# Cross-attention prologue: x loaded a second time with features on partitions, query weights centred on the chip, the layer norm's scale applied in the query eviction

## The reference, cut to what matters

```python
def _layernorm(x, axis=-1, eps=1e-05):
    m = jnp.mean(x, axis=axis, keepdims=True)
    v = jnp.var(x, axis=axis, keepdims=True)
    return (x - m) / jnp.sqrt(v + eps)
...
q = rms_norm(linear(h, q_w, q_b), norm_q_w)
...
x = x + _L0_xattn_ref(_layernorm(x, axis=-1), ctx_2048, ...)
x = x + _L0_ffn_ref(_layernorm(x, axis=-1), ...)
```

## Time and profile before

| | us |
|---|---|
| median of three runs (1572.07 to 1576.45) | 1574.91 |
| the profiled execution, its own time | 1576.47 |
| its span | 1574.7 |
| TensorE busy | 1532.1 (97%) |
| VectorE, ScalarE, GpSimd busy | 1190.8, 711.5, 702.1 |

### The profile page before, as it was taken

How to read it: one execution, slowest core, us unless ns; L and a number is a source line. 1 busy time by engine, 2 the same in 40 slices (tenths; PEclk the granted TensorE clock), 3 DMA queues, 4 the chain that set the end, 5 groups by cost and what they waited for, 6 DMA issues and landing times.

```text
span 1574.7 us, 41288 instructions
## 1 busy us (share of the span) xinstructions
PE 1532.1 (97%) x16250; PEld 1192.2 (76%) x16250; DVE 1190.8 (76%) x1884; ACT 711.5 (45%) x1457; POOL 702.1 (45%) x786
## 2 busy tenths in 40 slices
PE   8999999999999999999999999999997999999997
PEld 6776777777777777777777777777775787777997
DVE  5763788878888888888878888788888586554986
ACT  5763444443444444444434444434445124555441
POOL 5762444344444344444344443444446592113752
PEclk9999999999999999999999999999999999999999
DMA  6853111112211112111122111122114524011000
GB/s 190 238 161 128 47 55 56 49 49 70 70 49 55 49 51 78 60 50 53 49 66 69 54 54 49 49 69 71 49 36 125 190 107 161 27 36 46 1 1 24
DMA packets 66167, 113.70 MB, mean 72 GB/s; under 512 B 21392, under 2 KB 36080, under 8 KB 64576
## 3 DMA queue, kind: packets, MB, share of 16 engines
q1 hardware_dynamic: 65280, 110.20, 22.1%
q0 software_dynamic: 832, 2.75, 0.6%
HBM read 82.59 MB, written 30.34 MB: 72 GB/s over the span
## 4 chain that ended last, share of the span: by engine, by line
PE 90%; ACT 6%; DVE 2%; issue 1%; POOL 1%; DMA 0%; SPq 0%; ACTq 0%
PE ps L1466 22%; PE ps L1467 19%; PE ps L1468 19%; PE ps L1607 8%; PE ps L1573 6%; PE ps L1548 3%; PE ps L1519 3%; PE ps L1579 2%; PE ps L1818 2%; ACT prob L801 2%; PE ps L1801 2%; PE ps L1810 1%; PE ps L1501 1%; ACT prob L799 1%; PE ps L1583 1%
## 5 line engine op out<-in xcount | busy, mean ns | idle before, releaser
L547 POOL TENSOR_TENSOR prob_img<-prob 128x448 f32<-128x448 f32 x128 | 150.8, 1178 | 216.1 <-ACT prob L801 216.1
L510 POOL TENSOR_TENSOR ctx_lo<-ctx_raw,ctx_hi 128x472 fp32r<-128x472 f32 (+1 forms) x62 | 111.6, 1819 | 244.5 <-ACT ctx_hi L742 244.5
L1108 DVE RECIPROCAL rec<-ps 128x224 f32<-128x224 f32 x128 | 199.0, 1555 | 6.0 <-PE ps L1607 2.3
L799 ACT ACTIVATE prob<-ps 119x448 f32<-119x448 f32 x128 | 69.7, 545 | 196.0 <-PE ps L1573 196.0
L1097 DVE TENSOR_REDUCE top<-ps 112x4 f32<-112x1028 f32 x128 | 156.1, 1219 | 0.0
L1102 DVE SCALAR_TENSOR_TENSOR prob_img<-prob,ones_last,prob_img 23x448 f32<-23x448 f32 x128 | 87.5, 683 | 76.4 <-POOL prob_img L547 74.3
L775 ACT ACTIVATE sq_junk<-proj 128x513 bf16<-128x513 f32 (+1 forms) x96 | 61.1, 637 | 173.3 <-DVE proj L1076 173.3
L1096 DVE TENSOR_REDUCE top<-ps 112x4 f32<-112x472 f32 x128 | 82.9, 648 | 61.3 <-PE ps L1548 61.3
L1573 PE MATMUL ps<-q_all,k_all 32*128 32x112 f32 (+1 forms) x3072 | 125.7, 274 | 0.0
L801 ACT ACTIVATE prob<-ps 128x896 f32<-128x896 f32 x128 | 116.9, 914 | 0.0
L1466 PE MATMUL ps<-w_v_img_hi,ctx_hi 128*128 128x512 f32 x256 | 109.7, 428 | 0.0
(11 more groups left out here) (331 smaller groups left out, 4394.8 us busy)
## 6 DMA issues: line engine op xcount, KB each, us to landing
ctx_raw<-in_ctx_dram SPq DMA_DIRECT2D x32, 748.0 KB, 4.2
xh_dram<-xh SPq DMA_DIRECT2D x32, 448.0 KB, 3.1
q_dram<-q_turned SPq DMA_DIRECT2D x28, 256.0 KB, 2.8
q_all<-q_dram SPq DMA_DIRECT2D x32, 224.0 KB, 3.1
out_dram<-out_sb SPq DMA_DIRECT2D x32, 224.0 KB, 2.3
xh<-in_x_dram SPq DMA_DIRECT2D x31, 224.0 KB, 2.8
xa<-in_x_dram SPq DMA_DIRECT2D x21, 256.0 KB, 3.6
ring<-in_wo_dram SPq DMA_DIRECT2D x2, 2048.0 KB, 8.8
```

Source lines behind the costliest of these rows:

```text
L510: nc.gpsimd.tensor_tensor(ctx_lo[:, :, cols], ctx_raw[:, :, cols], ctx_hi[:, :, cols].bitcast(F32), ALU.subtract).then_inc(ctx_lo_done, 1)
L547: nc.gpsimd.tensor_tensor(prob_img[:, g % 2], prob[:, g % 2, 1, :], prob[:, g % 2, 2, :], ALU.add).then_inc(img_summed, 1)
L799: nc.scalar.activation(prob[0:CHUNK_C, g % 2, 0, :].rearrange("p (j q) -> p j q", j=GH), ps[0:CHUNK_C, 2:6, 0:L], ACT.Exp).then_inc(exp_do ...
L1108: nc.vector.reciprocal(rec[:], bank[:, 2:4]).then_inc(norm_step, 1)
```

## The change

The host program also passes `xT`, x with features on partitions, one tile of 128 tokens contiguous for each partition. SP loads it to one of three buffers `xc`, besides the rows, which go to one of two buffers `xa` and serve only for mean and variance. The turns of x, the GpSimd normalisation and its shift are gone. TensorE makes the mean of the query weights over features by four full-precision products with a constant of 1/512; VectorE subtracts it from the staged weights (`centre`). The eviction of a query tile multiplies by the token's inverse spread and adds the bias. The query turn of tile k-2 stands between the two halves of the products of tile k; ScalarE's copy of it comes one iteration later, behind the squares of tile k-1. The expansions of `pick_rows` move from the start to k = 12 and 14.

```diff
-        xa = [qp(f"xa{e}", [P, D])[:] for e in range(3)] + [proj[:, 1, 0:D]]
+        xc = [qp(f"xc{e}", [P, D])[:].rearrange("p (c l) -> p c l", c=KC) for e in range(3)]
+        xa = [proj[:, e, 0:D] for e in range(2)]
+        mean_w = q_turned[0][:, 0, :]
...
+            def load_xc(t_):
+                sp.dma_start(xc[t_ % 3], t["xT"][t_]).then_inc(xc_loaded[t_ % 3], 16)
...
             def pre():
                 sp.sem_inc(out_stored, 16)
+                load_piece(0)
+                load_xc(0)
+                load_piece(1)
                 load_xa(0)
+                sp.dma_start(pick_rows[:], t["pick_rows"]).then_inc(pick_loaded, 16)
+                load_xc(1)
+                sp.dma_start(q_bias[:], t["q_b"].partition_broadcast(P)).then_inc(q_bias_loaded, 16)
                 load_xa(1)
...
+                load_xc(2)
...
                 for k in range(NT + 2):
-                    if k + 4 < NT:
-                        sp.wait_ge(xT_full, k + 1)
-                        load_xa(k + 4)
+                    if k + 3 < NT:
+                        sp.wait_ge(xT_lo_done, k + 1)
+                        load_xc(k + 3)
+                    if k + 2 < NT:
+                        sp.wait_ge(ln1_step, 2 * k + 1)
+                        load_xa(k + 2)
...
-                pool.wait_ge(ln1_fixed, 3 * t_ + 3)
-                nc.gpsimd.tensor_scalar(xa[t_ % 4], xa[t_ % 4], tile_rstd[:, col], tile_shift[:, col], ALU.mult, ALU.add).then_inc(xa_ready, 1)
...
             def x_hi(t_):
-                act.wait_ge(xT_full, t_ + 1)
+                act.wait_ge(xc_loaded[t_ % 3], 16 * (t_ // 3) + 16)
                 if t_ >= 2:
                     act.wait_ge(qp_full, t_ - 1)
-                nc.scalar.activation(xT_hi[t_ % 2][:], ps[:, 6, :].rearrange("p (c l) -> p c l", c=KC), ACT.Copy).then_inc(xT_hi_done, 1)
+                nc.scalar.activation(xT_hi[t_ % 2][:], xc[t_ % 3], ACT.Copy).then_inc(xT_hi_done, 1)
...
+                    if k >= 2:
+                        q_copy(k - 2)
+                    if k == 12:
+                        act.wait_ge(pick_loaded, 16)
...
                     if k:
                         q_scale(k - 1)
-                        q_copy(k - 1)
                 squares(0, 1)
+                q_copy(NT - 1)
...
             def add_q_bias(t_):
                 dve.wait_ge(qp_full, t_ + 1)
                 if t_ >= 2:
                     dve.wait_ge(q_turn_full, t_ - 1)
-                nc.vector.tensor_tensor(q_row[t_ % 2][:, 0:D], (bank0, bank1)[t_ % 2], q_bias[:], ALU.add).then_inc(qp_done, 1)
+                dve.wait_ge(ln1_fixed, 2 * t_ + 2)
+                nc.vector.scalar_tensor_tensor(q_row[t_ % 2][:, 0:D], (bank0, bank1)[t_ % 2], tile_rstd[:, t_:t_ + 1], q_bias[:],
+                                               ALU.mult, ALU.add).then_inc(qp_done, 1)
...
+                def centre(j):
+                    rows = stage[:, j, :].rearrange("p (c o) -> p c o", c=2)
+                    dve.wait_ge(mean_full, 1)
+                    nc.vector.tensor_tensor(rows, rows, ps[:, 6, :].unsqueeze(1).to_broadcast([P, 2, D]), ALU.subtract).then_inc(centred, 1)
+
+                x_rest(0)
                 ln1(0)
+                centre(0)
+                centre(1)
+                piece(0)
+                piece(1)
                 ln1(1)
-                piece(0)
-                x_rest(0)
-                piece(1)
-                ln1(2)
                 for k in range(NT):
                     if k + 1 < NT:
                         x_rest(k + 1)
-                    if k + 3 < NT:
-                        ln1(k + 3)
+                    if k + 2 < NT:
+                        ln1(k + 2)
...
+            def weight_means():
+                for j in range(2):
+                    pe.wait_ge(piece_loaded[j], 16)
+                    for c in range(2):
+                        last = nc.tensor.matmul(ps[:, 6, :], mean_w, stage[:, j, c * D:(c + 1) * D], start=j + c == 0, stop=j + c == 2)
+                last.then_inc(mean_full, 1)
...
+                weight_means()
+                first_queries()
+                for k in range(1, NT):
+                    queries(k, 0)
+                    if k >= 2:
+                        turn_q(k - 2)
+                    queries(k, 1)
```

More of the change, by code:

```diff
@@ L122, in build @@
         tile_mv = p1("tile_mv", [P, NT, 2])
-        tile_var, tile_rstd, tile_shift, tile_sq, tile_inv = (p1(f"tile_{n}", [P, NT]) for n in ("var", "rstd", "shift", "sq", "inv"))
+        tile_var, tile_rstd, tile_sq, tile_inv = (p1(f"tile_{n}", [P, NT]) for n in ("var", "rstd", "sq", "inv"))
         sq_junk = p1("sq_junk", [P, D + 1], BF16)
@@ L1474, in project @@
                 return last
-            def turn_x(t_):
-                pe.wait_ge(xa_ready, t_ + 1)
-                if t_:
-                    pe.wait_ge(xT_lo_done, t_)
-                for c in range(KC):
-                    last = nc.tensor.transpose(ps[:, 6, c * P:(c + 1) * P], xa[t_ % 4][:, c * P:(c + 1) * P], ident[:])
-                last.then_inc(xT_full, 1)
-            def queries(t_, halves=range(2)):
-                pe.wait_ge(xT_lo_done, t_ + 1)
-                if t_ >= 2:
-                    pe.wait_ge(qp_done, t_ - 1)
-                bank = (bank0, bank1)[t_ % 2]
-                for half in halves:
-                    if t_ == 0:
-                        pe.wait_ge(piece_lo, half + 1)
-                    last = project(bank, xT_hi[t_ % 2], xT_lo[t_ % 2], slice(0, P), "q", range(2 * half, 2 * half + 2))
-                if 1 in halves:
-                    last.then_inc(qp_full, 1)
+            def weight_means():
[4 more added lines that the diff above has]
+                last.then_inc(mean_full, 1)
@@ new lines, in queries, with first_queries @@
+            def queries(t_, half):
+                if half == 0:
+                    pe.wait_ge(xT_lo_done, t_ + 1)
+                    if t_ >= 2:
+                        pe.wait_ge(qp_done, t_ - 1)
+                made = project((bank0, bank1)[t_ % 2], xT_hi[t_ % 2], xT_lo[t_ % 2], slice(0, P), "q", range(2 * half, 2 * half + 2))
+                if half:
+                    made.then_inc(qp_full, 1)
+            def first_queries():
+                pe.wait_ge(xT_lo_done, 1)
+                for kc in range(KC):
+                    if kc % 2 == 0:
+                        pe.wait_ge(piece_hi, kc // 2 + 1)
+                    nc.tensor.matmul(bank0, xT_hi[0][:, kc, :], w_hi["q"][:, kc, :], start=kc == 0, stop=False)
+                    nc.tensor.matmul(bank0, xT_lo[0][:, kc, :], w_hi["q"][:, kc, :], start=False, stop=False)
+                for kc in range(KC):
+                    if kc % 2 == 0:
+                        pe.wait_ge(piece_lo, kc // 2 + 1)
+                    last = nc.tensor.matmul(bank0, xT_hi[0][:, kc, :], w_lo["q"][:, kc, :], start=False, stop=kc == KC - 1)
+                last.then_inc(qp_full, 1)
@@ L1627, in pre @@
                 keys(0, 0)
-                turn_q(NT - 1)
+                turn_q(NT - 2)
                 pe.wait_ge(qp_done, NT)
                 keys(0, 1)
+                turn_q(NT - 1)
                 keys(0, 2)
@@ L1922 @@
         "x": c(a["x"]),
+        "xT": c(a["x"].reshape(NT, P, KC, P).transpose(0, 3, 2, 1)),
         "ctx": c(ctxT[:, :, order].reshape(B, KC, P, CTXC).transpose(0, 2, 1, 3)),
```

64 lines of the change are left out of this document (25 added, 39 removed).

## The result

The changed kernel took 1583.45 us (median of 5 runs, 1582.59 to 1585.74), the kernel before 1574.36 (median of 5): ratio 1.0062, 95% interval 1.0047 to 1.0077, so about 9 us slower. The profiled execution took 1582.62 us with a span of 1580.8.

A forecast was written before the change was run, and what follows sets the result against it. TensorE bound the kernel before; the change was to pass the query stage's pace to xa's loads. Steps of 8.7 and 7.3 us plus norm rows and bursts gave +8.5, taken as +8: 1574.9 + 8 = 1583 us, range 1570 to 1593.

The forecast's parts named there:

- Start: Start of the query stage, up to tile 1's products: shift 0, bounds -3 and +2 us.
- The loop: Query stage: copy, store, xc, xa, statistics, eviction, squares, copy over two tiles; 8.7 us even, 8.45 odd, 7.3 without pieces.
- odd chain: Loop over odd query tiles, with VectorE's 1.14 us rest of the weight piece: 8.45 us per two tiles.
- Landing of xa: Loads of rows in the loop: about 4.5 us after the store's issue, 4.9 with a weight piece behind; bounds 3.8 and 5.6.
- the bursts: Loads of norm rows, biases and first context among tiles 9 to 17, delaying xa: +3 us over four even steps.
- even chain: Loop over even query tiles, with ScalarE's 0.95 us weight piece: 8.7 us per two tiles, the slower chain.
- The sum: Query stage along the slower chain: eviction 4 at 34.4, eviction 24 at 123.6, keys at 131.1; shift +8.5, taken as +8.
- Tiles without pieces: Query tiles from tile 20, without weight pieces: the loop takes 7.3 us per two tiles.
- Keys at 131.1: End of the query stage: keys begin at 123.6 + 7.5 = 131.1 us, against 123.05 before.
- TensorE stays the pace: Rival for the query stage: 3.30 us a tile, 14 to 17 us faster, 1558 to 1561; chance 0.08.
- Short landings: Rival: same loop, xa landing 3.8 to 4.0 us after the store, no bursts; 1571 to 1575 us; chance 0.24.
- a cooled TensorE: Rival: waits drop TensorE's clock in the query stage, tiles some 5.5 to 6 us, time past 1610; chance 0.03.

The follow-up runs named there:

- e1: The changed kernel with four buffers for the rows xa, asked for four tiles ahead instead of two; 1575.16 us.
- e5: The changed kernel with ScalarE's copy of the turned queries put ahead of the squares and the weight piece; 1575.32 us.
- e3: The changed kernel with the loads of xa put ahead of those of xc in SP's queue; 1579.23 us.
- e4: The changed kernel with one more unused 256 KB load per tile between xc and xa; 1596.82 us.
- e8: The changed kernel with four xa buffers asked for four tiles ahead, and weight pieces asked for one SP iteration earlier; 1560.61 us.
- e9: The changed kernel, two xa buffers kept, with the weight pieces alone asked for one SP iteration earlier; 1585.45 us.
- e2: The changed kernel with the query stores issued from ScalarE's queue behind its copy instead of by SP; 1574.04 us.
- e6: The kernel before the change with only the query turns moved between product halves and ScalarE's copy one iteration later; 1568.78 us.
- c1: The changed kernel with both four xa buffers asked for four tiles ahead and query stores on ScalarE's queue; 1571.12 us.
- e7: The kernel before the change with one more unused 256 KB load per tile ahead of xa in SP's queue; 1579.27 us.

## Why the prediction was right, point by point

- **Start, 0.** Tile 1's products begin at 17.04 (17.08 before). Right.
- **The loop.** Its members and their order are as forecast; e1, e5, e3 and e4 each move the time by touching one member. The fixed steps of the odd chain were 3.95 us; measured, 9.18 less a mean of 5.23 is 3.95. Two tiles take 9.18 us along the odd chain and 9.10 along the even one, the upper edge of the 8.2 to 9.2 that I gave.
- **Landing of xa, 4.5 us after the store on odd turns.** In the eight odd turns from 33.08 it was 4.50, 5.19, 5.84, 4.57, 5.75, 4.71, 5.60 and 5.68, mean 5.23; behind the last piece 4.35 to 4.49. The first, second and fourth have no other load right behind the rows: mean 4.75, near the term. Behind the other five SP queues norm rows, biases, the first context or, at k = 19, small tables: mean 5.52. So most of what this chain took beyond the forecast came with the bursts, which the sum had only along the even chain.
- **The sum, along the even chain.** Evictions 4 to 20 were to take 8 x 8.7 + 1.4 + 3 = 74.0 us; they took 107.53 - 34.77 = 72.8. Two terms were mis-sized. Five of the eight steps took 8.23 to 8.46, mean 8.34: with a piece behind them the rows landed 4.43 to 4.61 us after the store, not 4.9. The other three (to evictions 10, 14 and 16) took 11.74, 10.35 and 8.98, together 6.0 over that mean, where bursts and norm rows had 4.4; the rows of the first landed 7.51 us after the store, behind the norm rows' loads. The errors have opposite signs, so that the total came so close is partly luck. Eviction 20 was to end at 108.4 and ended at 107.5; eviction 24 at 123.6, measured 123.3.
- **Tiles without pieces, 7.3 per pair.** 7.21 and 7.35.
- **Keys at 131.1.** 131.64; one of the last query turns waited 0.8 us for ScalarE's scaling (129.75), which I had not counted. The total, +9.1 against the +8 taken.
- **"TensorE stays the pace", 3.30 us a tile and 14 to 17 us.** Not what happened, but its size was right: e8 has 3.24 us in a tile without waits and takes 14 us less than before. Its own condition fell, though: xa need not land within 2.8 us, it may take 5.2, if nothing waits for it.
- **Short landings.** The fit of the Trainium skill ("DMA: Bandwidth & Descriptors", section "Anatomy of one DMA") is for one DMA on GpSimd's path; the estimate worked out from it puts the third of three 256 KB transfers 3.8 us after the first issue. The shortest store to statistics here was 4.35 (106.55 to 110.90). The measurement decides against this rival.
- **What the pieces cost in the loop.** Counted as work on VectorE and ScalarE, rightly for this kernel (e9). The second loop through their landing was missed; it changed nothing in the prediction, and it would have spoiled a forecast of the obvious repair, as it did mine for e1. The third, through the rest of x, was missed too, and with it e2 and e5.
- **The moved query turn.** I gave it no part of its own. e6 shows 5.7 of the 14 us of e8; the other 8.2 lie between e6 and e8, which differ in the turns of x (and in the centring, the scale in the eviction and the loads). The change as made lost both, and 9 us more.

## What to carry to other kernels

Before a buffer ring is made shallower, write down for each load what its issue waits for in the queue's program order, and follow that to the load's reader and back: here a landing of 5.2 us cost nothing outside such a loop (e8) and one of the same length was paid inside it. When one loop is cut, look for the next longest before naming a gain: e1, e2 and e5 each came out near 1575, e1 held by the pieces, e2 and e5 by the rest of x. And the remedy need not reduce work or bytes; asking one iteration earlier did it.

## What the runs showed of the hardware

The forecast weighed a cooled TensorE as a rival of 3 in 100 for the whole stage. It came, in spots. TensorE in the changed kernel behind its longest wait:

```profile
59.85 0.80 PE L1486 MATMUL ps<-w_q_hi,xT_hi 128*128 128x512 f32 x1 [2.95 <-DVE xT_lo L1074]
60.45 0.63 PE L1487 MATMUL ps<-w_q_lo,xT_hi 128*128 128x512 f32 x1
60.88 0.63 PE L1488 MATMUL ps<-w_q_hi,xT_lo 128*128 128x512 f32 x1
...
63.44 0.40 PE L1487 MATMUL ps<-w_q_lo,xT_hi 128*128 128x512 f32 x1
63.68 0.39 PE L1488 MATMUL ps<-w_q_hi,xT_lo 128*128 128x512 f32 x1
```

The products start 0.43 us apart, and 0.24 apart from 63.44 on: the lower clock level (1.2 GHz) and the higher (2.4). The granted clock of the three stretches 50.68 to 60.47, 60.47 to 69.00 and 106.55 to 113.76 was 0.95, 0.85 and 0.76; the wait of 0.96 us in the earlier trace rows had no such sequel. In the change this looks free, since the statistics after it still waited for the DMA (1.20 us at 65.04, 2.23 at 110.90). In e1 the stretch from 60 to 90 us had a clock of 0.83 behind waits of 3.39 and 2.86 us. In c1, above, two tiles at the lower level took 2.75 us more each than those at the higher; and over its ten runs the time goes with the mean granted clock, from 1566.92 us at 0.996 and 1568.81 at 0.995 to 1573.56 at 0.990 and 1576.21 at 0.989. This speaks for a cost of some us there; no run set the clock apart from the waits ahead of its fall.

The queues carried 323 to 343 GB/s over 30 us each with loads landing in 4.9 to 5.2 us (medians over both, e8), and 333 GB/s in e7 without slowing TensorE, whose tiles took 3.83 to 4.01 us as before.
